# The attention pass of a graph network on one core: float32 products against half-word products

## What is computed

```python
    def _L2_gnn_ref(feat, attention, src, dst, weight, h_bias):
        ...
        h = feat @ weight + h_bias
        m = h[src] * attention
        out = jax.ops.segment_sum(m, dst, num_segments=feat.shape[0])
        return out

    def _L3_gnn_ref(x, edge_index, W, b):
        ...
        for _ in range(K):
            h = jax.ops.segment_sum(norm[:, None] * h[src], dst, num_segments=n)
        return h @ W + b
```

## Time and profile before

| | |
|---|---|
| time, median of three runs | 9792.43 us |
| the profiled execution: its time | 9772.61 us |
| the profiled execution: its span | 9770.7 us |
| PE busy, of the span | 56% |
| GpSimd busy | 45% |
| DVE busy | 32% |
| ACT busy | 13% |
| DMA | 115 GB/s mean |

### The profile page before, as it was taken

How to read it: one execution, slowest core, us unless ns; L and a number is a source line. 1 busy time by engine, 2 the same in 40 slices (tenths; PEclk the granted TensorE clock), 3 DMA queues, 4 the chain that set the end, 5 groups by cost and what they waited for, 6 DMA issues and landing times.

```text
span 9770.7 us, 158177 instructions
## 1 busy us (share of the span) xinstructions
PE 5455.2 (56%) x59671; PEld 4646.5 (48%) x59671; DVE 3081.5 (32%) x5287; ACT 1301.1 (13%) x1613; POOL 4417.4 (45%) x4341
## 2 busy tenths in 40 slices
PE   6999767743333333335623555545445556776777
PEld 6999556732212212214522444434344445666667
DVE  6999211111111111115842223323222332111111
ACT  4777300000000000004620000000000000000000
POOL 2111043336666666666626555555555533333332
PEclk9999878876666666668956666666666677887888
DMA  4444245543323323325611222222222235555555
GB/s 134 181 181 183 90 144 174 178 117 82 86 74 84 81 77 86 81 77 170 196 33 36 74 73 73 72 66 72 72 75 74 72 95 172 183 181 177 179 176 169
DMA packets 615332, 1123.66 MB, mean 115 GB/s; under 512 B 208798, under 2 KB 420768, under 8 KB 602032
## 3 DMA queue, kind: packets, MB, share of 16 engines
q1 hardware_dynamic: 226720, 727.38, 23.0%
q10 hardware_dynamic: 253712, 248.81, 8.0%
q0 software_dynamic: 134432, 140.53, 7.2%
HBM read 857.81 MB, written 258.51 MB: 114 GB/s over the span
## 4 chain that ended last, share of the span: by engine, by line
issue 30%; PE 28%; another core or an unknown queue 15%; PEld 5%; DVE 5%; DMA 2%; ACT 1%; DVEq 1%; POOL 1%; SPq 0%; ACTq 0%; PEldq 0%; POOLq 0%
PE banks L891 11%; PE banks L1046 9%; PEld banks L891 5%; PE banks L1056 4%; DVE oneh L1107 1%; PE banks L1659 1%; DVE area L1964 1%; DMA area<-edge_h 1%; DVE oneh L1973 1%; PE banks L1678 1%; PE banks L581 1%; PE banks L569 0%; PE banks L1650 0%; POOL area L1314 0%
## 5 line engine op out<-in xcount | busy, mean ns | idle before, releaser
L389 POOL DMA_INDIRECT gath<-tab_l,idx x3328 | 3154.2, 948 | 2518.1 <-issue 1078.3
L921 POOL DMA_INDIRECT wide<-near_rows,kept x798 | 845.2, 1059 | 1898.0 <-PE banks L901 1144.9
L1659 PE MATMUL banks<-area,ones 128*128 128x448 f32 (+1 forms) x1040 | 582.7, 728 | 1372.6 <-DVE area L1964 1149.0
L1046 PE MATMUL banks<-area 128*128 128x128 f16 x4802 | 582.6, 252 | 952.4 <-issue 950.7
L1659 PEld LDWEIGHTS banks<-area,ones 128*128 128x128 f32 x1040 | 275.6, 276 | 1648.6 <-issue 1632.9
L1046 PEld LDWEIGHTS banks<-area 128*128 128x128 fp8e4 x4802 | 368.5, 110 | 1149.8 <-issue 1144.8
L1056 PE MATMUL banks<-oneh,gath 128*64 128x128 f32 x3328 | 576.0, 351 | 417.8 <-DMA gath<-tab_l,idx 359.4
L1964 DVE TENSOR_TENSOR area<-gath,banks 128x448 f32<-128x448 f32 (+1 forms) x256 | 138.7, 583 | 2008.6 <-remote 1463.1
L1056 PEld LDWEIGHTS banks<-oneh,gath 128*64 128x64 f32 x3328 | 541.1, 187 | 441.1 <-DMA gath<-tab_l,idx 364.8
L891 PE MATMUL banks<-wide,oneh 128*128 128x128 f16 x8232 | 572.1, 228 | 260.9 <-issue 260.1
L854 ACT CAST wide<-banks 128x784 uint16<-128x784 f32 x784 | 651.3, 859 | 222.1 <-PE banks L811 222.1
(11 more groups left out here) (274 smaller groups left out, 6576.2 us busy)
## 6 DMA issues: line engine op xcount, KB each, us to landing
gath<-counts SPq DMA_DIRECT2D x252, 784.0 KB
oneh<-counts SPq DMA_DIRECT2D x252, 784.0 KB
counts<-wide SPq DMA_DIRECT2D x98, 1568.0 KB, 5.2
gath<-counts ACTq DMA_DIRECT2D x98, 784.0 KB
area<-counts ACTq DMA_DIRECT2D x98, 784.0 KB
area<-edge_feat SPq DMA_DIRECT2D x128, 448.0 KB
gath<-tab_l,idx POOLq DMA_INDIRECT x3328
edge_h<-area ACTq DMA_DIRECT2D x128, 416.0 KB
```

The lines of the kernel that those rows point to most:

```text
L389: pool.indirect_dma_start(out=to[:, h, c, 0:H], out_offset=None, in_=table[:, :], in_offset=bass.IndirectOffsetOnAxis(ap=idx[:, slot, c:c ...
L921: pool.indirect_dma_start(out=pick_rows[k][r][:, c, :], out_offset=None, in_=near_rows[k][:, :], in_offset=bass.IndirectOffsetOnAxis(ap=pi ...
L1046: last = T.matmul(to, part_in[u].bitcast(f8)[:, t, s * P:(s + 1) * P], block_rows[:, k % 2, s, :, :].rearrange("p a f -> p (a f)"), start= ...
L1659: ins = T.matmul(bank[n][:, 0:(hi - lo) * H], ones[:, :], src[:, lo:hi, :].rearrange("p c f -> p (c f)"), start=first and lo == 0, stop=la ...
```

## The change

The gathered rows are weighed instead of the one-hots. DVE waits for a group's rows and multiplies them by the attention (`weigh`, L1169, 128 x 832); ACT scales them into a 16-bit high half (`high_of_group`, L1029); DVE subtracts it for the low half (L1173). Both halves stand side by side in `both`, so that one product (128 weights wide) sums high and low at once against the byte one-hots `att_oh`, which SP now loads from `edge_oh` for every group. The scale comes from a bound of |h|, worked out once ahead of the pass (`a_top`, 15 small steps on PE, DVE and ACT). `add` takes 128 x 128 instead of 64 x 128, the block's sums are turned by node against `w_norm[:, 0, :]`, which adds the halves (`sums_by_node`). The row slot is free once its low half is made (`s_lo`) and no longer when the group is summed. `add(q)` moves behind `weigh(q + 1)`. The high half makes ACT work through the groups too, so the `part_load`s are moved between them: the two of a step stand behind that step's high half.

```diff
-        def early_act(act, b, k, groups):
-            part_load(act, b, 0)
-            part_load(act, b, 1)
+        def unscaled_sums(b, h):
+            return S.activation(sta[:, h, :], blk(feat, 0, P, b), ACT.Identity, scale=bn[:, 3, 0:1])
+
+        def early_act_steps(act, b, k, groups):
             hold(act, p_att.added, groups + 2)
-            l2_steps(act, b, [(1, sums_to_sta), *ln_act(4), (11, keep_resid), (15, keep_block(k))])
+            l2_steps(act, b, [(1, unscaled_sums), *ln_act(4), (11, keep_resid), (15, keep_block(k))])
+
+        def high_of_group(act, q, h):
+            hold(act, s_weighed, q + 1)
+            hold(act, p_att.summed, q + 3)
+            S.activation(both[:, h, :, 0, :], near[:, h, :, :], ACT.Identity, scale=scale[:, 0, 0:1]).then_inc(s_hi, 1)
+
+        def early_act(act):
+            def step(b, k, st, groups):
+                if st == 0:
+                    early_act_steps(act, b, k, groups)
+                elif st <= NB // 2:
+                    for j in (2 * st - 2, 2 * st - 1):
+                        part_load(act, b, j)
...
+            with act.Fori(0, EARLY // 2) as i:
+                for s in range(2 * EACH):
+                    q = BEFORE + 2 * EACH * i + s
+                    high_of_group(act, q, s % 2)
+                    step(2 * i + s // EACH, s // EACH, s % EACH, q)
...
         def att_group(pe, q, k, h):
             hold(pe, p_att.added, q + 1)
-            hold(pe, p_att.onehot, q + 1)
-            pe.wait_ge(p_att.rows_in[h], 16 * C * (k + 1))
+            hold(pe, s_oh[h], OH_BASE + 16 * (k + 1))
+            hold(pe, s_lo, GROUPS + 3 + q)
             for c in range(C):
-                last = T.matmul(window[h][0:H, :], near[:, h, c, :], oneh[:, h, c, :], start=(c == 0), stop=(c == C - 1))
+                last = T.matmul(window[h], both[:, h, c, :, :].rearrange("p a f -> p (a f)"), onehots_of(att_oh[h])[:, c, :],
+                                start=(c == 0), stop=(c == C - 1))
             last.then_inc(p_att.summed, 1)
...
-            def place(q, h):
-                at = bass.ds(q, 1)
-                V.tensor_copy(group_w[:, h, 0, :], dst_f[:, at, :].rearrange("p a c -> p (a c)"))
-                V.tensor_copy(group_w[:, h, 1, :], att_s[:, at, :].rearrange("p a c -> p (a c)")).then_inc(s_weighed, 1)
-                hold(dve, s_weighed, q + 1)
-                hold(dve, p_att.summed, q + 3)
-                for c in range(C):
-                    ins = V.tensor_scalar(oneh[:, h, c, :], iota_p, group_w[:, h, 0, c:c + 1],
-                                          group_w[:, h, 1, c:c + 1], ALU.is_equal, ALU.mult)
-                ins.then_inc(p_att.onehot, 1)
+            def weigh(q, k, h):
+                dve.wait_ge(p_att.rows_in[h], 16 * C * (k + 1))
+                V.tensor_tensor(near[:, h, :, :], near[:, h, :, :],
+                                att_s[:, bass.ds(q, 1), :].rearrange("p a (c o) -> p (a c) o", o=1).to_broadcast([P, C, H]),
+                                ALU.mult).then_inc(s_weighed, 1)
+                hold(dve, s_hi, GROUPS + q + 1)
+                V.scalar_tensor_tensor(both[:, h, :, 1, :], near[:, h, :, :], scale[:, 0, 0:1], both[:, h, :, 0, :],
+                                       ALU.mult, ALU.subtract).then_inc(s_lo, 1)
...
             with dve.Fori(0, EARLY // 2) as i:
                 for s in range(2 * EACH):
                     q = BEFORE + 2 * EACH * i + s
-                    add(q, s % 2)
-                    place(q + 2, s % 2)
+                    weigh(q, BEFORE // 2 + EACH * i + s // 2, s % 2)
+                    add(q - 1, 1 - s % 2)
                     step(2 * i + s // EACH, s // EACH, s % EACH)
...
+                        hold(sp, s_lo, GROUPS - 1 + q)
+                        sp.dma_start(idx[:, s, :], group(src_idx, q)).then_inc(idx_in[s], 16)
+                        hold(sp, p_att.summed, q + 3)
+                        sp.dma_start(att_oh[s % 2], group(edge_oh, q)).then_inc(s_oh[s % 2], 16)
...
-                gather(pool, p_att, n_win, 1, tab_l2, p_att.summed, (before, 1), to=near)
+                gather(pool, p_att, n_win, 1, tab_l2, s_lo, (before, 1), to=near, plus=GROUPS - 2)
```

More of the change, by code:

```diff
@@ L231, in gnn_program @@
         block_rows = sta[:, 0, :].bitcast(f16).rearrange("p (u t a f) -> p u t a f", u=2, t=TB, a=2)
+        both = flat_of(oneh)[:, 0:2 * C * H].bitcast(f16).rearrange("p (s c a f) -> p s c a f", s=2, a=2, f=H)
+        att_oh = [flat_of(oneh)[:, 2 * C * H + s * C * W // 4:2 * C * H + (s + 1) * C * W // 4] for s in range(2)]
+        OH_BASE = 16 * ITERS + 16 + 16 * (ITERS // 2)
         FEW = 10
@@ new lines, in high_of_group @@
+        def high_of_group(act, q, h):
[9 more added lines that the diff above has]
+                        part_load(act, b, j)
+            act.wait_ge(a_top, 5)
+            S.activation(bn[:, 1, 1:2], bn[:, 1, 0:1], ACT.Sqrt, bias=eps[:, :], scale=float(H)).then_inc(a_top, 1)
+            act.wait_ge(a_top, 15)
+            with act.Fori(0, BEFORE // 2) as i:
+                for h in range(2):
+                    high_of_group(act, 2 * i + h, h)
+            with act.Fori(0, EARLY // 2) as i:
[3 more added lines that the diff above has]
+                    step(2 * i + s // EACH, s // EACH, s % EACH, q)
+            for s in range(EACH - 1):
+                q = BEFORE + EACH * (EARLY - 1) + s
+                high_of_group(act, q, q % 2)
+                step(EARLY - 1, EARLY - 1, s, q)
+            part_load(act, EARLY, 0)
+            part_load(act, EARLY, 1)
+            early_act_steps(act, EARLY, EARLY, GROUPS)
@@ L1137, in step @@
                         part_added(b, j)
-            for q in range(2):
-                place(q, q)
             V.memset(sums_a, 0.0).then_inc(s_pre, 1)
             V.memset(sums_b, 0.0).then_inc(s_pre, 1)
-            dve.wait_ge(s_pre, 9)
-            with dve.Fori(0, BEFORE // 2) as i:
+            dve.wait_ge(s_pre, 8)
+            weigh(0, 0, 0)
+            weigh(1, 0, 1)
+            add(0, 0)
+            with dve.Fori(1, BEFORE // 2) as i:
                 for h in range(2):
-                    add(2 * i + h, h)
-                    place(2 * i + h + 2, h)
+                    weigh(2 * i + h, i, h)
+                    add(2 * i + h - 1, 1 - h)
             with dve.Fori(0, EARLY // 2) as i:
```

82 lines of the change are left out of this document (56 added, 26 removed).

## The result

| | before | after |
|---|---|---|
| median on one chip | 9787.22 us (4 runs) | 10066.58 us (4 runs, 10063.23 to 10070.63) |
| ratio | | 1.0285, 95% interval 1.0272 to 1.0298 |
| the profiled execution's span | 9770.7 us | 10068.8 us |
| PE, DVE, ACT, GpSimd busy | 56, 32, 13, 45% | 52, 28, 14, 44% |
| mean granted clock of PE | 0.746 | 0.717 |

The change makes the kernel 2.85% slower, 279 us between medians and 298 us between the two profiled spans. By its share of the span every engine but ACT is less busy. That kernel's median was 9770 to 9787 us on the chips used, but 9681 us on one, that of four runs (the shorter gather, both edits together, and the two that weigh first); why is not known, so ratios from that chip and from the others are compared only with care.

What follows compares the result with a forecast made beforehand. PE gets little done while rows are gathered, so each step is a chain tied to the gather's end. +86 (steps) +16 (block changes) -20 (first groups) = +82 us, 9855 profiled, 9875 us as median; range 9650 to 10115 us.

Steps and rivals of the forecast that it cites:

- P to S, the restart chain: From a step's second product's end (P) to the next gather's start (S): 6.1 us against 5.3, 0.8 us worse.
- S to P: From a gather's start (S) to the step's second product's end (P): 20.1 us against 19.8, 0.3 us worse.
- step: Steady part, one gather start to the next: 26.2 us, +1.1 us in each of 78 periods, +86 us.
- change of block: Change of block with its first step: mean 64.5 us (61 early, 75 late) against 63.2; +16 us over 12.
- first groups, scale steps: First twelve groups: 20 us gained, sums having 26 records instead of 52; steps for the scale, under the second gather: 0.
- product one still runs freely: A step's first product: two loads keep the gather's first packets back until about 6 us, so it runs freely.
- nearest: Of bounds 18.5 and 22.8 us from gather start to second product's end, today's 19.8 was called nearest.
- the early case: At a change of block, DVE goes on 18.2 us after the turn by node is issued; taken three times in four.
- its cover: At a change of block, GpSimd's two gathers (32.5 us) cover weighing placed behind the layer norm; if lost, 75 us.
- the loads come too late: Rival: products start inside PE's slow stretch under a gather; 22.8 us to second product's end, +324 us, 10117 us; chance 0.21.
- The gather has no hold on PE: Rival: slow products come from something the change removes; products end 10 us after gather's start; -800 us, 8990 us; chance 0.07.

Runs made afterwards that it cites:

- the shorter gather: Kernel before, with a group's gather fetching only 7 of its 13 sets of rows; ratio 0.8977.
- both edits together: Changed kernel, with loads of counts issued a step ahead and the next group weighed before the second part product is added; ratio 1.0110.
- the two that weigh first: Changed kernel, next group weighed ahead of both part products' sums; gather waits for the sum two groups back (ratio 0.9734) or for the low half (0.9952).
- the gather behind the sum: Changed kernel, with loads of counts a step ahead and the gather waiting for the sum two groups back instead of the low half; ratio 1.0213.
- the run with the lists first: Changed kernel, with SyncE issuing a group's index list ahead of the one-hots of the group two before; ratio 1.0271.
- early loads: Changed kernel, with the loads of counts issued a step ahead again; ratio 1.0219.
- the run with the early gather: Changed kernel, with the next group weighed ahead of both part products' sums and the gather still waiting for the low half; ratio 0.9952.
- Fillers: 40 products of constants before each group's sum behind a step with products: changed kernel, ratio 1.0261; with loads a step ahead too, 1.0208.

## Why the prediction was right in its direction and wrong in its size

| term | forecast | measured |
|---|---|---|
| P to S, the restart chain | 6.1 us | 6.0 us |
| S to P | 20.1 us | 21.6 to 21.8 us |
| step | 26.2 us, +86 | 27.8 us, +211 |
| change of block | 64.5 us, +16 | 69.1 us, +71 |
| first groups, scale steps | -20, 0 | -10, +7 |
| sum on the profiled execution | +82 us | +298 us |

**The restart chain** was right to 0.1 us, and each of its links to 0.15 us. That GpSimd now waits for links for which it had not waited is the case's main point; the float32 sum's 4.5 us was traded for them, and with most of them off the path the time was that of before (ratio 1.0003).

**The step that failed** is "I take 20.1 us, 0.3 us worse". It rested on two sentences: that the two loads would hold the gather's packets back so that "product one still runs freely", and that today's 19.8 is "nearest". Product one did run freely, but what mattered was how many records were through before S. The runs put a price on each part: 0.8 us for the loads (21.8 to 21.0), some 1.3 us for the head start of sum and product one together (21.0 to 19.65 with the gather behind the sum), 0.1 to 0.2 us for the clock. The prediction had written that the new sum "starts when the gather starts, and so leaves the path", and booked its removal as a gain. It left the path on paper; the head start that the old order had given product one left with it. 1.6 us x 78 = 125 us of the missing 216.

**The change of block** is the second mis-sized term. The signal came 3 to 8 us after the start of L1097 in ten of twelve cases, more often than three in four and more than ten us sooner than the early case had it; but it won nothing, since GpSimd was busy with two gathers meanwhile. The third began at 5783.32, 40.4 us after the last product, where the prediction's terms come to 41.1: right, but set by the gathers and not by the signal. The third low half (L1173 at 5773.62) was there before the second gather was through, so GpSimd ran three gathers without a pause, and the step's first product began among them. The prediction called the two gathers "its cover" and gave the first step the usual 20.1 us; from 5783.32 to the second product's end (5805.90 + 4.98) it took 27.6. In the mean of the twelve changes 4.6 us were missing, 55 us in all.

The first twelve groups were foretold without idle time on GpSimd. It stood there for SyncE's lists, 33 us in three pieces, and would have stood as long for the low half, as the run with the lists first shows. SyncE's extra loads were put at nothing because they are issued a group ahead; that the lists behind them in the queue come late was not considered. The 20 us of gain were taken because a sum has 26 records instead of 52; but one wait only took the place of another, which had been 32 us in six pieces before. The 10 us ahead of the pass are no part of any term.

Of the rivals, "the loads come too late" (step 28.9, 10117 us) was nearest in time, yet its mechanism is not what happened in the steps: the products did not start in the slow stretch, and early loads gave back only 0.8 of the 2.0 us that S to P lost. Only at the changes of block did product one begin so late. That the time lies within the stated range, 9650 to 10115 us, is owed to this rival's price and is luck. "The gather has no hold on PE" fell with the shorter gather. The Trainium skill says on its page SBUF — State Buffer, section Who interferes with whom, that "DMA never contends with a compute engine". That speaks of SBUF's ports, and no run here tests those; but whoever takes it to mean that DMA leaves PE alone is wrong for this kernel: the runs show a gather's calls and PE's pace and signals tied together, though not through which part of the chip.

## What to carry to other kernels

Where a GpSimd gather slows PE, count the records that PE gets through ahead of the gather's start: a wait moved to an earlier releaser can win nothing (1.0219 and 1.0213), and one made longer can win 2.2%. An operation that goes from the side of a chain into its links is paid in full, however cheap it is for its engine; look for the order in which its inputs are ready a step early. In a queue worked in order, the place of a load has a price though its bytes stay the same (0.8 us a step for the loads of counts).

## What the runs showed of the hardware

- PE gets a number of products through once a gather starts, and then slows down. It ran 54 products freely in the median, both where product one started 0.7 us behind S and where it started 2.5 us behind, up to 5.3 and 7.7 us after S, so it was the count that ended and not a time; from 0.9 to 1.0 us ahead of S it ran 68 to 71. The number is not the same everywhere: in five steps before the change in which product one started 7.0 us behind S it was 44 or 45. Then the products come slowly, in the median step 20 in 15.3 us before the change and 14 in 10.9 us after it.
- The release lags behind the last call by more the longer GpSimd has issued without a pause: 1.5 us after 7 calls, 2.5 after 13, 4.3 after 26 (6236.44 to 6240.79 in the run with the early gather), 5.1 after 39 (5799.24 to 5804.35), and up to 6.7 at the other changes of block. In the longest stretch the products came 2.8 us apart.
- A product's signal waits likewise: product one's was seen 18.9 us after S, with the release, where it had started behind S, and 8.9 us after S where it had started ahead of it.
- PE did the products that are left after a release at the lower level of its clock (1.2 GHz), before the change as after it: the granted clock was 0.50 from 6021.0 to 6022.3 us there and from 6331.0 to 6335.0 here. In product one it was 1.00 before the change (6003.2 to 6005.8) and 0.50 after it (6315.0 to 6317.5), where PE had stood idle for 5.3 us ahead of the sum and for 1.6 us behind it. Fillers raised the clock and hardly moved the time.

Through which part of the chip a gather holds PE stays open; no run here tried to tell it. One thing can be read from the trace before: the queue that carries instructions moved one packet of 16 KB between 6001 and 6003 us, and none between 6004 and 6021 us, the slow stretch of that step. That speaks against a supply of instructions that trickles, and does not rule out one that is held up.
